# Scan steps of a unit shifted by two slots, and rank sums taken in quarters of the rows

## The reference

```python
# layer 0: linear retention with decay 0.96875 ** (i - j), and a five-matrix FFN
scores = einsum('bid,bjd->bij', q, k) * D          # causal, no softmax
s = einsum('bij,bjd->bid', scores, v)
h = silu(w1 x) * (w2 x); h = gelu(h1 h); h = gelu(h2 h)
x = x + s * silu(w3 h)
# layer 1: a state-space scan over time (128 features x 16 states) ...
x_conv = silu(causal depthwise conv of 4 taps(xn @ W_in[:, :128]))
h = A * h + xc_t[:, :, None] * B_t[:, None, :]
y = einsum('bn,bdn->bd', C_t, h) + D_param * xc_t
s = (y * silu(gate)) @ W_out + b_out
# ... and a mixture-of-depths FFN: the better half of the tokens by router score
top_scores, top_idx = top_k(einsum('bsd,d->bs', xn, w_router), S // 2)
g = xn; g[top_idx] += sigmoid(top_scores) * (gelu(xn[top_idx] @ W1 + b1) @ W2 + b2)
x = x + s * silu(g)
```

## Time and profile before

| what | us |
|---|---|
| median of 3 runs | 546.79 (545.92 to 547.64) |
| the profiled execution | 545.56 |
| span of its instructions | 543.8 |
| busy: PE, DVE, POOL, ACT | 443.4, 407.9, 404.7, 291.4 |
| mean granted TensorE clock | 0.95 of full speed |

### The profile page before, as it was taken

One profiled execution on the slowest core, in us unless ns is written; L12 is line 12 of the kernel. 1 busy time (PEld: TensorE's weight loads), 2 busy tenths in 40 slices (PEclk: granted clock), 3 DMA queues, 4 the chain that ended last, 5 costly groups with the idle time before them and its releaser, 6 DMA issues.

```text
span 543.8 us, 6040 instructions
## 1 busy us (share of the span) xinstructions
PE 443.4 (82%) x1777; PEld 259.0 (48%) x1791; DVE 407.9 (75%) x659; ACT 291.4 (54%) x475; POOL 404.7 (74%) x316
## 2 busy tenths in 40 slices
PE   0796978898889897989899888989798999485743
PEld 0575645644564455545565456445554464131211
DVE  2282144959788977989598959898789779958985
ACT  3664736774567545763676366745676447313300
POOL 1673543887599959985999769985999599855582
PEclk9997979899999999999999999999999999978865
DMA  8300006311513143221532162214321332215220
GB/s 316 136 20 4 1 0 175 85 51 40 155 60 86 50 125 108 77 77 47 152 96 78 37 176 77 79 39 118 115 79 58 96 99 78 78 44 165 85 74 19
DMA packets 25379, 46.97 MB, mean 86 GB/s; under 512 B 3072, under 2 KB 4096, under 8 KB 25088
## 3 DMA queue, kind: packets, MB, share of 16 engines
q1 hardware_dynamic: 24336, 45.13, 28.1%
q10 hardware_dynamic: 1008, 1.41, 0.8%
HBM read 42.33 MB, written 4.19 MB: 86 GB/s over the span
## 4 chain that ended last, share of the span: by engine, by line
POOL 35%; DVE 23%; issue 17%; PE 16%; ACT 5%; DMA 1%; SPq 0%; DVEq 0%; POOLq 0%; ACTq 0%
POOL hs L548 15%; DVE hs L1359 10%; PE bank0a L932 7%; DVE xbank L1336 7%; POOL hidAl L510 6%; POOL hidBl L510 5%; PE bank1a L1012 2%; POOL xnTl L492 2%; POOL g L526 2%; POOL g L522 2%; DMA Bt<-w_in 1%; POOL xr L530 1%; POOL q L499 1%; PE ybank L1071 1%; DVE st L1262 1%
## 5 line engine op out<-in xcount | busy, mean ns | idle before, releaser
L548 POOL TENSOR_TENSOR hs<-hs,Ct 128x512 f32<-128x512 f32 x127 | 184.6, 1459 | 32.6 <-DVE hs L1359 19.7
L510 POOL TENSOR_TENSOR hidAl<-plain,hidAh 128x512 fp32r<-128x512 f32 x48 | 64.6, 1346 | 37.7 <-ACT hidAh L643 31.3
L1359 DVE TENSOR_TENSOR_SCAN hs<-decay,carry,xbank 128x512 f32<-128x512 f32 x63 | 80.5, 1278 | 7.6
L510 POOL TENSOR_TENSOR hidBl<-plain,hidBh 128x512 fp32r<-128x512 f32 x48 | 66.1, 1378 | 26.6 <-ACT hidBh L643 18.7
L1359 DVE TENSOR_TENSOR_SCAN hs<-decay,xbank 128x512 f32<-128x512 f32 x64 | 78.0, 1219 | 5.6 <-DVE xbank L1336 0.5
L1336 DVE TENSOR_TENSOR xbank<-xs,bbank 128x512 f32<-128x512 f32 x104 | 71.4, 687 | 1.3
L642 ACT ACTIVATE plain<-bank0a,col 128x512 f32<-128x512 f32 x64 | 44.2, 690 | 45.2 <-PE bank0a L932 44.0
L932 PE MATMUL bank0a<-hidBh,hTh 128*128 128x512 f32 x128 | 57.7, 451 | 1.7 <-ACT q L675 1.7
L932 PE MATMUL bank0a<-hidAh,hTh 128*128 128x512 f32 x128 | 57.0, 445 | 1.7 <-ACT q L675 1.7
L932 PE MATMUL bank0a<-hidAl,hTh 128*128 128x512 f32 x128 | 51.6, 403 | 0.0
L932 PE MATMUL bank0a<-hidBl,hTh 128*128 128x512 f32 x128 | 50.7, 396 | 0.0
(11 more groups left out here) (184 smaller groups left out, 951.7 us busy)
## 6 DMA issues: line engine op xcount, KB each, us to landing
xs<-x_rows SPq DMA_DIRECT2D x128, 256.0 KB, 3.4
xt<-x_tok SPq DMA_DIRECT2D x8, 256.0 KB, 4.5
xr<-x_feat SPq DMA_DIRECT2D x8, 256.0 KB, 7.6
x_rows<-xc SPq DMA_DIRECT2D x8, 256.0 KB, 2.0
out<-xr SPq DMA_DIRECT2D x7, 256.0 KB, 2.2
fh<-h_w SPq DMA_DIRECT2D x1, 1024.0 KB, 10.0
hs<-h_w SPq DMA_DIRECT2D x1, 1024.0 KB, 11.9
lw<-l_w ACTq DMA_DIRECT2D x1, 640.0 KB, 5.4
```

The lines of the kernel that those rows point to most:

```text
L510: pool.tensor_tensor(low[:, m, :], plain[:, k % NPLAIN, :], high[:, m, :].bitcast(F32), ALU.subtract).then_inc(hidden_low, 1)
L548: pool.tensor_tensor(h, h, Ct[:, hs_(u)], ALU.mult).then_inc(p_ready, 1)
L1359: dve.tensor_tensor_scan(hs[:, i % NSTATES, :], decay[:, gr:gr + 1].broadcast_to([P, HALF]), xbank[:], 0.0 if u % 2 == 0 else carry[:, k:k ...
```

## The change

1. LEAD becomes 10: step k of a unit stands two slots later for every engine. With it move `gather_y(t,1)` from slot 1 to 3, `gather_y(t,2)` from 4 to 6, `gather_y(t,3)` from 8 to 10, `gather_y(n,0)` from 14 to 15 (there behind the last two `mod_up`), `gate_y` from 9 to 12, the last unit's `finish_last` and `project_last` by two, and `keep_B` from 8 to 11. The end of the kernel has two slots more.
2. SyncE spreads rows four steps ahead across the border of units, one step to a slot, instead of four at once in slot 6.
3. For all units but the last, the eight rank products become: four products of 32 columns for the four own tiles in slot 7, each into its own quarter of the rows of `bank1d`; four more on top in slot 12; ScalarE's `take_parts`, which writes the sums, scaled by 1/32, as bfloat16 over `ffn`; and one product by ones over all rows in slot 13 (`rank_total`). `token_weights` moves to slot 13 and `add_tokens` to 14. `take_ffn` now waits for the rank before.

```diff
-LEAD = NGRP // 2
+LEAD = 10
...
-    return (1, 1, 1, 1, 1, 1, 1, 1) if u == UNITS - 1 else (7, 7, 9, 9, 12, 12, 12, 12)
+    return (1, 1, 1) if u == UNITS - 1 else (7, 12, 13)
...
-    return 2 if u == UNITS - 1 else 12
+    return 2 if u == UNITS - 1 else 13
...
-    return 2 if u == UNITS - 1 else 13
+    return 2 if u == UNITS - 1 else 14
...
-                if n is not None and s == 6:
+                if n == 0 and s == 6:
                     for k in range(NROWS - 1):
-                        spread_x(n, k)
+                        spread_x(0, k)
                 u, k = scanned(p, s)
-                if u is not None and k + NROWS - 1 < NGRP:
-                    spread_x(u, k + NROWS - 1)
+                if u is not None and step(u, k + NROWS - 1) <= LAST:
+                    spread_x(*divmod(step(u, k + NROWS - 1), NGRP))
...
+            def take_parts(t):
+
+                act.wait_ge(ranked, (t + 1) * CH)
+                act.wait_ge(ffn_weighed, t + 1)
+                act.activation(parts, bank1d[:], ACT.Copy, scale=CPH / P).then_inc(parts_taken, 1)
...
+                if t is not None and t < UNITS - 1 and s == rank_slots(t)[1]:
+                    take_parts(t)
...
                     elif s == 8:
                         score_columns(n)
-                        keep_B(n)
...
+                if n is not None and s == 11:
+                    keep_B(n)
...
+                    for j in range(CPH):
+                        pe.matmul(bank1d[j * P // CPH:(j + 1) * P // CPH, :], ones[:, 0:P // CPH],
+                                  beats[:, i * CPH + j, :], start=(i == 0), stop=(i == 1)).then_inc(ranked, 1)
+
+                def rank_total(u):
+                    pe.wait_ge(parts_taken, u + 1)
+                    pe.matmul(bank1d[:], ones[:], parts, start=True, stop=True).then_inc(l1_dve_full, 1)
...
-                    if s in (1, 4) and t is not None:
-                        gather_y(t, 1 if s == 1 else 2)
+                    if s in (3, 6) and t is not None:
+                        gather_y(t, 1 if s == 3 else 2)
...
-                    if s == 8 and t is not None:
+                    if s == 10 and t is not None:
                         gather_y(t, 3)
...
-                    if t == UNITS - 1 and s == 9:
+                    if t == UNITS - 1 and s == 11:
                         project_last()
...
-                    if n is not None and s == 14:
+                    if n is not None and s == 15:
                         gather_y(n, 0)
...
-                    if t == UNITS - 1 and s == 8:
+                    if t == UNITS - 1 and s == 10:
                         finish_last()
-                    elif t < UNITS - 1 and s == 9:
+                    elif t < UNITS - 1 and s == 12:
                         gate_y(t)
```

More of the change, by code:

```diff
@@ L262, in program @@
         ffn = sb("ffn", [P, HALF])
+        parts = ffn[:, 0:HALF // 2].bitcast(BF16)
         xc = sb("xc", [P, SEQ])
@@ L343, in program @@
         ranked = sem("ranked")
+        parts_taken = sem("parts_taken")
         ffn_full = sem("ffn_full")
@@ L754, in take_ffn @@
                 if t > 0:
-                    act.wait_ge(ffn_weighed, t)
+                    act.wait_ge(l1_dve_full, done(L1_DVE, ("rank", t - 1)))
                 act.wait_ge(ffn_full, t + 1)
@@ L1029, in score_column, with rank_quarters @@
                     last.then_inc(l1_act_full, 1)
-                def rank(u, pos):
-                    r = u * CH + pos
-                    if pos == 0:
+                def rank_quarters(u, i):
+                    if i == 0:
                         open1d(("rank", u))
@@ L1037, in rank @@
                             pe.wait_ge(ffn_taken, u + 1)
-                    pe.wait_ge(beats_ready, r + 1)
-                    pe.matmul(bank1d[:], ones[:], beats[:, r % NBEATS, :], start=(pos == 0),
-                              stop=(pos == CH - 1)).then_inc(l1_dve_full if pos == CH - 1 else ranked, 1)
+                    pe.wait_ge(beats_ready, u * CH + (i + 1) * CPH)
+                    if u == UNITS - 1:
+                        for j in range(CPH):
+                            c = i * CPH + j
+                            pe.matmul(bank1d[:], ones[:], beats[:, c, :], start=(c == 0),
+                                      stop=(c == CH - 1)).then_inc(l1_dve_full if c == CH - 1 else ranked, 1)
+                        return
+                    for j in range(CPH):
+                        pe.matmul(bank1d[j * P // CPH:(j + 1) * P // CPH, :], ones[:, 0:P // CPH],
[3 more added lines that the diff above has]
+                    pe.matmul(bank1d[:], ones[:], parts, start=True, stop=True).then_inc(l1_dve_full, 1)
                 def mod_up(t, m):
@@ L1098, in slot @@
                     if t is not None:
-                        for pos in range(CH):
-                            if rank_slots(t)[pos] == s:
-                                rank(t, pos)
+                        for i in range(2):
+                            if rank_slots(t)[i] == s:
+                                rank_quarters(t, i)
+                        if t < UNITS - 1 and rank_slots(t)[2] == s:
+                            rank_total(t)
                     if v is not None and s < KT:
@@ L1292, in compare @@
                 dve.wait_ge(l1_act_done, done(L1_ACT, ("score_col", u // 2 * 2 + c // CPH)))
[L1293 to L1297, removed]
+                if u > 0:
+                    dve.wait_ge(ranked, (u - 1) * CH + pos + 1)
                 s_i = scol[:, u // 2 % 2, c:c + 1]
@@ L1312, in compare_other @@
                 if u > 0:
-                    full1(("rank", u - 1))
+                    dve.wait_ge(ranked, u * CH)
                 s_i = scol[:, u // 2 % 2, cs_(other)].rearrange("p (c o) -> p c o", o=1)
```

## The result

| | before | changed |
|---|---|---|
| median of 4 runs each, us | 546.95 | 589.07 (583.93 to 592.01) |
| ratio, 95% interval | | 1.0762 (1.0684 to 1.0839) |
| the profiled execution, its span | 545.56, 543.8 | 588.99, 587.2 |
| mean granted TensorE clock | 0.950 | 0.903 |

The change costs 42.1 us, about twice the 20.6 that were forecast, and the time lies above the range.

The account below looks back on a forecast made before the run. No engine alone but a ring through VectorE, TensorE, GpSimd and ScalarE bounds each period; 16.5 us for p = 1 to 5, 2.8 for p = 6, 0.3 and 1.0 at the ends make +20.6: 566 us, 80% range 550 to 572.

Parts of the forecast that it names:

- (a): From VectorE's residual_l0 through slots 0 to 3 and TensorE's outer to GpSimd's start; that start comes 0.8 us earlier.
- (c): TensorE's chain from hidden("h2",0) through w3, gate and residual_l0; net +0.1 to +0.2 us per period.
- The ring: One period between residual_l0 starts as three stretches, VectorE and TensorE, then GpSimd, then TensorE and ScalarE; +3.1 or +3.6 us.
- S: GpSimd's start after its idle of 5.16 us, at 259.36 in period 3 before; forecast 0.8 us earlier.
- Stretch (b): GpSimd without pause; k = 15 weighed 16.75 us after its start, 2.1 of it for compare_other; hidden("h2",0) +3.8 or +4.3.
- 0.45 more for odd t: Further delay of GpSimd before k = 15 is weighed, in odd-t periods: +3.6 us per period against +3.1 for even t.
- p = 0 and the tail: The ends of the kernel: +0.3 us in p = 0, +1.0 from p = 7 on.
- p = 6: Last of the six periods, without norm or rstd: hidden("h2",0) +4.8, less 0.8 and 1.24; +2.8 us.
- rival 4: The four rank quarters don't overlap: 0.65 us more in slot 12, 570 us; counted within the forecast's 0.70.
- Rival 1: VectorE comes to compare_other only after k = 15 is weighed: 552 us, range 549 to 558; chance 0.12.
- Rival 2: Ring unchanged, GpSimd weighs k = 15 within 13.7 us of its start without any delay: 546 us; chance 0.07.
- Rival 3: Faster: gather in slot 10 finds k = 15 done within 12.9 us of GpSimd's start: 540 us; chance 0.11.

Follow-up runs that it names:

- e5: Changed kernel with compare_other in slot 12 behind gate_y and the other compares one slot later: 570.09 us, 1.0426.
- e3: Changed kernel with gather_y(t,3) one slot later, behind the first h2 pass, hidden("h2",0): 568.27 us, 1.0424.
- e2: Kernel before (LEAD 8) with only the rank products in column quarters added: 544.82 us, 0.9973.
- e1: Changed kernel with the ranks of the kernel before, so the shift by two slots alone: 583.25 us, 1.0689.
- e9: Changed kernel with rstd_l0 in slot 7 instead of 8, gather_y(t,3) and gate_y in slot 12, gather_y(t,1) in slot 2: 547.87 us, 1.0060.
- e6: Changed kernel with gather_y(t,1) in slot 2 instead of 3: 577.42 us, 1.0613.
- e11: Changed kernel with rstd_l0 in slot 7, gather_y(t,3) and gate_y in 12, gather_y(t,1) in 2, gather_y(n,0) back in 14: 553.71 us, 1.0169.
- e4: Changed kernel with 18 unread products filling TensorE's idle time behind retention_out in slot 9: 582.16 us, 1.0661.
- e10: Changed kernel with gather_y(t,3) behind hidden("h2",0), compare_other behind gate_y, gather_y(t,1) in slot 2, and 12 unread products in slot 9: 565.35 us, 1.0348.

## Why the prediction was wrong

The sign and the path through the engines held; the range failed, as one cost was put at nothing without a reason: what TensorE's clock does when its idle time grows. Both places where it fell are steps of the prediction, (a) and (c) below.

- **The ring**. Right: the chain of the changed kernel goes through S, GpSimd without a pause, the gather of quad 3 and h2, as it was laid out. The 1.77 of waiting for `hs` lies in the forecast 1.5 to 3.5; w3's wait for GpSimd is gone, and VectorE's waits for `Bt` fell from 22.6 us to 9.6, which is a single wait while the pipeline fills.
- **Stretch (b).** Right: S + 17.05 against 16.75, and e5 shows its two parts apart, 14.5 and the compare. The 0.45 more for odd t is right too: from S to h2(0) it is 19.40 and 19.41 in p = 2 and 4 (t odd), and 18.96 in p = 3 and 5, where all four were 13.97 before. The length of whole periods, 64.0 to 65.5, hides it.
- **Stretch (a), "S comes 0.8 us earlier".** The step failed by 1.2 us: S came 0.5 later. At full clock it is right, as e3 shows (25.06 for 25.3). What was not asked is what TensorE does without the gather in slot 1: it comes earlier to the z product of slot 2, waits 2.30 us there instead of 1.79, and the clock falls behind that wait.
- **Stretch (c), the gather's 1.05 and "to the end of w3 it took 273.33 to 291.1", taken over as they stood.** The step failed by 2.0: 0.9 on the gather, at 0.50 throughout, and 1.1 from h2(0) on. Of the 1.1, 0.8 are the two h2 passes (4.87 for 4.08), whose first products run at 0.50; the other 0.3 weren't taken apart. The prediction let TensorE wait for GpSimd and then go on at the speed of rows that had been read at a clock of 1.00. It also missed the idle time itself: it asked what the gather does in slot 10, and not what TensorE does without it in slot 8, with `norm_l0` late by 1.5 us, since the pow took 2.0 longer.
- **The sum.** Per period 1.2 in (a), 0.3 in (b) and 2.0 in (c) were missing, 3.5 of the 3.6 us by which period 3 exceeds its 61.7. Six times this is 21, of the 23 between 566 and 589. Counted over all six periods, S came 6.8 us later than forecast, h2(0) after S 7.4 and the next residual after h2(0) 8.9. The term for the clock was in neither the sum nor the range, and no rival had it.
- **p = 0 and the tail.** Right: +0.1 for 0.3, +1.0 for 1.0. p = 6 was +7.7 for 2.8, off in every stretch: S came 0.7 later instead of 0.8 sooner, h2(0) 6.5 later after S instead of 4.8, and the rest took 0.5 more where 1.2 less was forecast; the clock was 0.50 in slots 2 and 3 and again ahead of and in h2(0).
- **The ranks.** Right that the quarters overlap (rival 4 is out) and cost nothing (e2). VectorE's new wait for `bbank` is there, 5.26 for about 4, and covered, as forecast: it idles another 3.82 ahead of the residual.
- **The rivals.** Rival 1 is out, as `compare_other` started at S + 8.7, ahead of k = 15 (forecast S + 8.5). Rival 2 is out: GpSimd stands still for the compare even with a small pow. Rival 3 needed k = 15 within S + 12.9. It took 14.5 even with the compare away.

Open are why the clock falls behind a wait in one period and not behind the same wait in another, with it the 5.8 us between e1 and the changed kernel, and the 0.3 above. No version with LEAD = 10 came below the kernel before.

## What to carry to other kernels

When a step moves to another slot of an in-order queue, cost the slot that it leaves as well: an engine that arrives early at the next wait gains nothing, and TensorE may pay for the longer idle time by running the following products at half clock, here about 3 us a period, as much as all the costs forecast together. Before an instruction of one engine that blocks another is moved, list everything that stands in the blocked queue at that time, the small instructions that the critical chain hangs on first. Gains of experiments that relax the same gate don't add; ask after each which wait comes last now. And where a stretch repeats in a trace, compare its repeats before two kernels: they show what an edit did and what the clock did by itself.

## What the runs showed of the hardware

The length of a wait alone didn't tell whether the clock falls. In the changed kernel a wait of 2.15 us in slot 2 of p = 2 is followed by 0.50, and one of 2.14 at the same place of p = 4 by 1.00. In e9 a wait of 2.16 is followed by 0.50 in period 3, some 1.5 us after TensorE had gone back to work, and by 1.00 in period 5. With the gather moved into slot 2 (e6 to e11) the wait there was 1.1 or less and the clock fell behind it in none of the periods p = 1 to 6.

After it fell in these periods, 3 to 10 us passed at half clock, and products of 512 columns took 0.63 where they take 0.39. Products that nobody needs held the clock (0.66 for `retention_in` in e4 and e10 against 1.11), but in neither kernel did that shorten period 3 by more than 0.1, as it fell behind the next wait; in p = 1 of e4, where it didn't, h2(0) to the next residual took 18.8 instead of 20.4.
